# A gated recurrence: transfers of half the image, step by step, and a step's sums in units of 64 columns

## Chip, core and metric

The kernel runs on one core of a Trainium2 chip. The metric is the device time of one execution in microseconds. Five engines run their own instruction streams: TensorE (PE, with its weight loads as PEld), VectorE (DVE), ScalarE (ACT), GpSimd (POOL) and SyncE (SP, which here only issues transfers).

## What is computed

An attention layer and then a GRU, both with a residual, for 4 sequences of 512 positions with 512 features:

```python
x = x + attention_layer(x, cond)         # RMS norm, q, k, v, 16 heads, output projection
# GRU over the 512 positions of x, started from cond:
gi = x @ W_ih + b_ih                     # known for all positions in advance
gh = h @ W_hh + b_hh                     # needs the last state
r = sigmoid(i_r + h_r)
z = sigmoid(i_z + h_z)
n = tanh(i_n + r * h_n)
h = (1.0 - z) * n + z * h                # 512 steps, one after the other
out = x + hs
```

The state of a step is 4 x 512, the weights W_hh are 512 x 1536, all in 32-bit floats.

## The kernel before

The attention stage runs first, then the recurrence: T = 512 steps in N_BLK = 16 blocks of BLK = 32 steps. All engines run the same unrolled loop over the steps and meet through semaphores.

**A step on TensorE** (L490 to L501). The state is the stationary operand (4 columns), the weights stream as the moving one. Four column groups j of 32 columns work on four pieces of the output features side by side. `hidden_side` (L456) makes 8 matmuls for one half of the contraction (2 k by 4 j) over 128 columns; a matmul in 32-bit floats stands in the trace as two loads and two matmuls. The state comes in halves: A (features 0 to 255, semaphore h_a) and B (h_b). After h_a: the first half of the reset sums of all chunks, and of the update and candidate sums (zn) of the A chunks. After h_b: their second halves (r_sum, zna_sum), then both halves of zn for the B chunks (znb_sum). That is 6 calls. Sums are added onto PSUM banks that ScalarE's `seed` (L608) has filled with the input side and the biases, two steps ahead, in alternating triples of banks.

**A step on VectorE and ScalarE.** VectorE transposes the reset sums (L829), ScalarE makes r of them (L625 tanh, L628 affine). VectorE transposes zn of A (L809), adds i_n + r * h_n with a scan (L814), makes z from ScalarE's tanh (L634, L820), ScalarE takes the candidate's tanh (L636), and a scan (L824) writes the new A half. Then the same for B. VectorE's and ScalarE's queues run in this written order.

**The input side.** TensorE computes gi for the next block of 32 steps in pieces (`gi_piece`, L444), one piece after a step's sums, in 24 of 32 steps. VectorE evacuates it with the bias to `gi_image`, three operations of 128 columns for each of 4 sequences (L779, L781). SP writes the image to DRAM (`gi_spill`) and reads it back in another layout into `seeds`, a ring of 44 steps, of which `seed` takes one row set a step. `send_gi` (L202 on) does this once a block: one write of 1536 KB, then for two waves of 16 steps four reads each (8 where the ring wraps), 8 partitions by 16 steps by 1536 bytes. Half of each row set is padding: the candidate's input part stands on other partitions (rows B to 2B) than the rest. Finished blocks go to `out` by `send_rows`; TensorE turns their rows (L485) and ScalarE copies them (L614).

Of the kernel before, what the change touches and what calls it, by code (L numbers as in the profile page):

```python
# [49 lines left out]
RING = 44  # L50
# [4 lines left out]
WAVE = BLK // 2  # L55
# [3 lines left out]
def attention_gru_kernel(nc, x, cond, W_emb, b_emb, g_norm, W_qkv, g_q, g_k, W_out,  # L59
                         W_ih, W_hh, b_ih, b_hh, out):  # L60
    with ExitStack() as ctx:
# [75 lines left out]
        gi_image = sb("gi_image", [P, 2 * B, GCOL])  # L137
        gi_spill = nc.dram_tensor("gi_spill", (P, 2 * B, GCOL), F32, kind="Internal").ap()
# [7 lines left out]

        GI_BANKS, ROW_BANK = (6, 7), 7

        (ld_cond, ld_emb, ld_wqkv, ld_wout, ld_wih, ld_whh, ld_bias, ld_gi_early, ld_gi_late, ld_x, ld_g, st_gi, st_out) = (
            sem(n) for n in ("ld_cond", "ld_emb", "ld_wqkv", "ld_wout", "ld_wih", "ld_whh", "ld_bias", "ld_gi_early", "ld_gi_late",  # L150
# [8 lines left out]
            "bias_ready", "image_clear", "seeds_clear", "hid_n_ready", "pairs_ready", "banks_open", "gi_done", "gi_evac", "seeded", "h_a", "h_b",  # L159
            "r_sum", "zna_sum", "znb_sum", "rT_ready", "znaT_ready", "znbT_ready", "tr_done", "r_ready_gru", "va_done", "vb_done",  # L160
            "tza_done", "tzb_done", "za_done", "zb_done", "na_done", "nb_done", "out_added", "rows_ps", "rows_ready")}

        def step_banks(step):
            first = 3 * (step % 2)
            return first, first + 1, first + 2

        def seed_parts(wave):
            first = wave * WAVE % RING
            count = min(WAVE, RING - first)
            done = wave % 2 * WAVE  # L170
# [18 lines left out]
        def _(sp):  # L189
# [12 lines left out]
            def send_gi(n):  # L202
                sp.wait_ge(s["gi_evac"], 3 * B * (n + 1))
                if n > 0:
                    sp.wait_ge(ld_gi_early, gi_landed(2 * n - 2))
                    sp.wait_ge(ld_gi_late, gi_landed(2 * n - 1))
                sp.dma_start(gi_spill, gi_image[:]).then_inc(st_gi, 16)
                sp.wait_ge(st_gi, 16 * (n + 1))
                for wave in (2 * n, 2 * n + 1):
                    if n > 0:  # L210
                        sp.wait_ge(s["seeded"], (wave + 1) * WAVE - RING)
                    for first, done, count in seed_parts(wave):
                        for j in range(4):
                            sp.dma_start(seeds[QD * j:QD * j + 2 * B, first:first + count, :],
                                         gi_spill[QD * j + done:QD * j + done + count].rearrange("t r n -> r t n")
                                         ).then_inc(ld_gi[wave % 2], 16)

            def send_rows(m):
                sp.wait_ge(s["rows_ready"], KT * (m + 1))
                for b in range(B):  # L220
                    sp.dma_start(out[b, m * BLK:m * BLK + BLK, :], out_rows[BLK * b:BLK * b + BLK, :]).then_inc(st_out, 16)

            sp.wait_ge(s["seeds_clear"], 2)
            send_gi(0)
            for m in range(N_BLK):
                if m + 1 < N_BLK:
                    send_gi(m + 1)
                if m > 0:
                    send_rows(m - 1)
            send_rows(N_BLK - 1)  # L230
# [424 lines left out]
        def _(dve):  # L655
# [141 lines left out]
            for n, b in ((0, 0), (0, 1), (0, 2), (0, 3), (1, 0)):  # L797
                dve.wait_ge(s["gi_done"], B * n + b + 1)
                if n == 1:
                    dve.wait_ge(st_gi, 16)  # L800
# [90 lines left out]
```

## Time and profile before

| | us |
|---|---|
| median of 3 executions | 2526.01 |
| lowest, highest | 2499.19, 2531.39 |
| profiled execution | 2524.64 |
| its span in the trace | 2522.4 |
| TensorE busy | 2255.0 |
| VectorE busy | 1512.3 |
| ScalarE busy | 1245.4 |

The span runs from the first to the last recorded instruction; some 2 us lie outside it. Busy times can overlap, and a busy TensorE is not an array at its peak, since matmuls are pipelined. "Issue" as the reason of a wait means that the engine waited for nothing that the profile shows. DMA queues are numbered; the one called q8 has the kind "instruction".

### The profile page before, as it was taken

The numbers are of one execution on the slowest core, as the hardware profiler recorded it, in microseconds if no ns is written. First come the engines' busy times: TensorE is split into PE (matmuls) and PEld (weight loads), VectorE is DVE, ScalarE is ACT, GpSimd is POOL, SyncE is SP. The second block draws the span as 40 slices with busy tenths as digits, with TensorE's granted clock in tenths as the row PEclk, the third lists the DMA queues.
The fourth block names the chain that finished last, engine by engine and source line by source line (L and its number), as shares of the span: only waits on it lengthen the run. The fifth ranks groups of instructions, "written<-read, shape, count | busy, mean of one in ns | idle before, by whom it ended". The sixth has DMA issues, their size and how long they took to land.

```text
span 2522.4 us, 130844 instructions
## 1 busy us (share of the span) xinstructions
PE 2255.0 (89%) x58512; PEld 1764.2 (70%) x58512; DVE 1512.3 (60%) x5877; ACT 1245.4 (49%) x4666; POOL 199.8 (8%) x223
## 2 busy tenths in 40 slices
PE   5999999998679899989799897979898989979788
PEld 4756666575468687767678685868686778768676
DVE  3867868686256565646466564646565656546565
ACT  3757757574145444444345443545444445445454
POOL 3324232332000000000000000000000000000000
PEclk9999999999799999989899998999999999999999
DMA  5000000001220303021111303030302112030300
GB/s 192 2 18 1 2 17 2 1 2 51 52 53 5 58 5 58 29 33 36 25 41 22 54 9 53 9 57 5 58 32 30 37 25 49 14 55 7 58 4 12
DMA packets 33218, 80.23 MB, mean 32 GB/s; under 512 B 7696, under 2 KB 24080, under 8 KB 30608
## 3 DMA queue, kind: packets, MB, share of 16 engines
q1 hardware_dynamic: 26240, 63.97, 13.0%
q8 instruction: 460, 7.54, 1.3%
q0 software_dynamic: 1584, 7.73, 0.8%
q14 instruction: 102, 0.84, 0.1%
q10 hardware_dynamic: 4832, 0.15, 0.1%
HBM read 42.48 MB, written 29.36 MB: 28 GB/s over the span
## 4 chain that ended last, share of the span: by engine, by line
PE 77%; issue 8%; DVE 7%; ACT 6%; DMA 1%; ACTq 1%; POOL 0%; POOLq 0%; SPq 0%; DVEq 0%
PE ps L461 51%; PE ps L447 6%; PE ps L341 6%; PE ps L292 5%; PE ps L385 2%; PE ps L368 2%; DVE rT L829 2%; PE ps L327 2%; PE ps L434 2%; DVE xb L824 2%; ACT xb L636 1%; ACT r_pair L628 1%; ACT r_pair L625 1%; DVE v_pair L814 1%; ACT probs L595 1%
## 5 line engine op out<-in xcount | busy, mean ns | idle before, releaser
L461 PE MATMUL ps<-wqkv,xb 128*4 128x128 f32 x49152 | 1534.1, 277 | 192.4 <-issue 128.8
L461 PEld LDWEIGHTS ps<-wqkv,xb 128*4 128x4 f32 x49152 | 1240.0, 88 | 493.1 <-DVE xb L824 296.7
L829 DVE STREAM_TRANSPOSE rT<-ps 128x128 f32<-128x128 f32 x512 | 162.2, 317 | 495.5 <-PE ps L461 495.3
L625 ACT ACTIVATE r_pair<-rT 128x16 f32<-128x16 f32 x512 | 112.2, 219 | 653.4 <-DVE rT L829 653.4
L809 DVE STREAM_TRANSPOSE znT<-ps 128x128 f32<-128x128 f32 x1024 | 313.1, 306 | 90.3 <-PE ps L461 30.7
L634 ACT ACTIVATE t_z<-znT 128x8 f32<-128x8 f32 x1024 | 214.5, 209 | 280.1 <-DVE znT L809 279.8
L824 DVE TENSOR_TENSOR_SCAN xb<-z_trip,xb 128x24 f32<-128x24 f32 x1024 | 213.2, 208 | 121.5 <-ACT xb L636 3.6
L609 ACT ACTIVATE ps<-seeds 128x384 f32<-128x384 f32 x512 | 243.9, 476 | 60.3 <-DMA seeds<-gi_spill 60.3
L636 ACT ACTIVATE xb<-v_pair 128x16 f32<-128x16 f32 x1024 | 222.8, 218 | 52.7 <-DVE v_pair L814 0.9
L447 PE MATMUL ps<-wih,x1T 128*32 128x256 f32 (+1 forms) x4096 | 238.1, 328 | 11.3 <-issue 11.3
L814 DVE TENSOR_TENSOR_SCAN v_pair<-r_pair,znT 128x16 f32<-128x16 f32 x1024 | 196.3, 192 | 70.8 <-ACT r_pair L628 0.5
L820 DVE TENSOR_SCALAR z_trip<-t_z 128x8 f32<-128x8 f32 x1024 | 177.8, 174 | 26.5 <-ACT t_z L634 1.0
L341 PE MATMUL ps<-wqkv,xnT 128*128 128x384 f32 x512 | 192.7, 497 | 0.0
L595 ACT ACTIVATE probs<-ps,negmax 128x512 f32<-128x512 f32 x256 | 173.3, 686 | 19.5 <-DVE negmax L725 19.5
L725 DVE TENSOR_REDUCE negmax<-ps 128x1 f32<-128x512 f32 x256 | 158.4, 681 | 8.8 <-PE ps L368 8.8
L292 PEld LDWEIGHTS ps<-ident,probs 128*128 128x128 f32 x1024 | 117.1, 142 | 44.9 <-issue 17.2
L292 PE MATMUL ps<-ident,probs 128*128 128x128 f32 x1024 | 142.3, 279 | 4.0 <-ACT probs L595 3.7
L447 PEld LDWEIGHTS ps<-wih,x1T 128*32 128x32 f32 x4096 | 124.9, 111 | 18.8 <-issue 13.4
L628 ACT ACTIVATE r_pair<-r_pair 128x16 f32<-128x16 f32 x512 | 112.4, 219 | 16.2
L341 PEld LDWEIGHTS ps<-wqkv,xnT 128*128 128x128 f32 x512 | 87.0, 191 | 31.8
L272 POOL TENSOR_TENSOR qk_rs<-qk_ms,half_neg 128x8 f32<-128x8 f32 x64 | 106.7, 1667 | 12.1 <-POOL qk_ms L270 12.1
L729 DVE COPY probsT<-ps 128x512 f32<-128x512 f32 x128 | 82.6, 685 | 36.0 <-PE ps L292 34.3
(83 smaller groups left out, 1266.6 us busy)
## 6 DMA issues: line engine op xcount, KB each, us to landing
gi_spill<-gi_image SPq DMA_DIRECT2D x16, 1536.0 KB, 6.3
seeds<-gi_spill SPq DMA_DIRECT2D x92, 192.0 KB
xb<-in_x SPq DMA_DIRECT2D x4, 1024.0 KB, 5.7
out<-xb SPq DMA_DIRECT2D x64, 64.0 KB, 1.9
seeds<-gi_spill SPq DMA_DIRECT2D x24, 144.0 KB
wqkv<-in_L_cond_W_qkv SPq DMA_DIRECT2D x1, 3072.0 KB, 12.1
wih<-in_L_cond_W_ih POOLq DMA_DIRECT2D x1, 3072.0 KB, 16.4
wqkv<-in_L_cond_W_hh POOLq DMA_DIRECT2D x1, 3072.0 KB, 10.5
```

The source lines that it names most:

```text
L292: return nc.tensor.transpose(dst, src, ident[:])
L341: return nc.tensor.matmul(ps[:, pj(n), 0:3 * P], xnT[:, k, P * t:P * t + P], wqkv[:, k, :].rearrange("p (a g n) -> p a g n", a=3, g=G)[:, ...
L447: last = nc.tensor.matmul(ps[QD * j:QD * j + QD, bank, first:first + width], x1T[:, k, b, BLK * block_no:BLK * block_no + BLK], gate_cols( ...
L461: last = nc.tensor.matmul(ps[QD * j:QD * j + B, bank, 0:P], hist_flat[:, first:first + 3 * B - 2:3], weights, start=False, stop=False, ski ...
L595: nc.scalar.activation(probs[:, hh, :], ps[:, SC[hh], :], ACT.Exp, bias=negmax[:, m % 2, hh:hh + 1], accum_out=sums[:, m % 2, hh:hh + 1]). ...
L609: nc.scalar.activation(ps[:, 3 * (step % 2):3 * (step % 2) + 3, 0:P], seeds[:, step % RING, :].rearrange("p (u n) -> p u n", u=3), ACT.Cop ...
L634: nc.scalar.activation(t_z[:, half, :], znT[:, half, 0:16:2], ACT.Tanh, scale=0.5).then_inc(s[tz_name], 1)
L636: nc.scalar.activation(elements(step, half).rearrange("p (e s) -> p e s", s=3)[:, :, 0:3:2], v_pair[:, 8 * half:8 * half + 8, 1].unsqueeze ...
L809: return nc.vector.transpose(znT[:, half, :].rearrange("p (r k b s) -> p k r s b", r=4, k=4, b=B, s=2), ps[:, bank, 0:P])
L814: return nc.vector.tensor_tensor_scan(v_pair[:].rearrange("p e s -> p (e s)")[:, first:first + 16], r_pair[:].rearrange("p e s -> p (e s)" ...
L824: return nc.vector.tensor_tensor_scan(next_elements(step, half), z_trip[:].rearrange("p e s -> p (e s)")[:, 24 * half:24 * half + 24], ele ...
L829: nc.vector.transpose(rT[:], ps[:, r_bank, 0:P]).then_inc(s["rT_ready"], 1)
```

## The change

*Order of sums.* The step's sums are made in smaller units: reset for the A chunks and for the B chunks are apart (64 columns each), update and candidate of A stay together (128 columns), candidate of B and update of B are apart (64 each). After h_a: r_a, r_b and zn_a, first halves. After h_b: the second halves of r_a, zn_a, r_b, then both halves of n_b (after a wait for raT_ready) and of z_b (after a wait for znaT_ready), since they share a bank with sums that VectorE reads. These are 10 calls of `hidden_side`. VectorE transposes five pieces instead of three, and makes r of the B half itself (affine) from ScalarE's tanh. ScalarE takes the B half's update tanh last. `seed` becomes three copies of 128 elements.

*Image.* `gi_image` holds 4 rows instead of 8, without padding; one evacuation of 384 columns for each sequence. It is written to DRAM sequence by sequence (196 KB each), into one of two buffers. It is read back in four waves of 8 steps, one of the 16 pieces (wave, j) a step, each as two transfers (4 partitions by 8 steps by 1024 bytes, and by 512 bytes). The ring has 36 steps; its candidate part is filled with the hidden bias once. A block's output goes out one sequence a step.

```diff
-RING = 44
+RING = 36
 HIST = 16
 ENTRY = 3 * 17
 GCOL = 3 * P
 LEAD = 12
-WAVE = BLK // 2
+WAVE = 8
+FETCH_LEAD = 17
...
+        gi_spill = nc.dram_tensor("gi_spill", (2, B, P, GCOL), F32, kind="Internal").ap()
...
+        def gate_sums(step):
+            bank = 3 * (step % 2)
+            return {"zn_a": ps[:, bank, 0:2 * HP], "z_b": ps[:, bank, 2 * HP:3 * HP],
+                    "r_a": ps[:, bank + 1, 0:HP], "n_b": ps[:, bank + 1, HP:2 * HP], "r_b": ps[:, bank + 2, 0:HP],
+                    "r_both": ps[:, bank + 1:bank + 3, 0:HP], "n_both": ps[:, bank:bank + 2, HP:2 * HP],
+                    "z_both": ps[:, bank, 0:4 * HP].rearrange("p (h n) -> p h n", h=2)[:, :, 0:HP]}
...
-            def send_gi(n):
-                sp.wait_ge(s["gi_evac"], 3 * B * (n + 1))
-                if n > 0:
-                    sp.wait_ge(ld_gi_early, gi_landed(2 * n - 2))
-                    sp.wait_ge(ld_gi_late, gi_landed(2 * n - 1))
-                sp.dma_start(gi_spill, gi_image[:]).then_inc(st_gi, 16)
-                sp.wait_ge(st_gi, 16 * (n + 1))
-                for wave in (2 * n, 2 * n + 1):
-                    if n > 0:
-                        sp.wait_ge(s["seeded"], (wave + 1) * WAVE - RING)
-                    for first, done, count in seed_parts(wave):
-                        for j in range(4):
-                            sp.dma_start(seeds[QD * j:QD * j + 2 * B, first:first + count, :],
-                                         gi_spill[QD * j + done:QD * j + done + count].rearrange("t r n -> r t n")
-                                         ).then_inc(ld_gi[wave % 2], 16)
-
-            def send_rows(m):
+            def spill(n, b):
+                sp.wait_ge(s["gi_evac"], B * n + b + 1)
+                if n >= 2 and b == 0:
+                    for wave in range(4):
+                        sp.wait_ge(ld_gi[wave], gi_landed(n - 2, wave))
+                sp.dma_start(gi_spill[n % 2, b], gi_image[:, b, :]).then_inc(st_gi, 16)
+
+            def fetch(n, wave, j):
+                for first, done, count in seed_parts(n, wave):
+                    rows = slice(QD * j + done, QD * j + done + count)
+                    sp.dma_start(seeds[QD * j:QD * j + B, first:first + count, 0:2 * P],
+                                 gi_spill[n % 2, :, rows, 0:2 * P]).then_inc(ld_gi[wave], 16)
+                    sp.dma_start(seeds[QD * j + B:QD * j + 2 * B, first:first + count, 2 * P:3 * P],
+                                 gi_spill[n % 2, :, rows, 2 * P:3 * P]).then_inc(ld_gi[wave], 16)
...
+            for step in range(T):
+                m, u = divmod(step, BLK)
+                n, due = divmod(step + FETCH_LEAD, BLK)
+                if 1 <= n < N_BLK and due < 16:
+                    wave, j = divmod(due, 4)
+                    if due == 0:
+                        sp.wait_ge(st_gi, 16 * B * (n + 1))
+                    sp.wait_ge(s["seeded"], step + 2)
+                    fetch(n, wave, j)
+                ahead, due = divmod(step + LEAD - 7, BLK)
+                if ahead + 1 < N_BLK and due % 6 == 0 and due < 6 * B and step + LEAD - 7 >= 6:
+                    spill(ahead + 1, due // 6)
...
-                        last = nc.tensor.matmul(ps[QD * j:QD * j + B, bank, 0:P],
-                                                hist_flat[:, first:first + 3 * B - 2:3], weights,
+                        last = nc.tensor.matmul(into[QD * j:QD * j + B], hist_flat[:, first:first + 3 * B - 2:3], weights,
...
-                hidden_side(r_bank, R_GATE, ALL_CHUNKS, step, 0)
-                hidden_side(zna_bank, ZN_GATES, CHUNKS_A, step, 0)
+                hidden_side(into["r_a"], R_GATE, CHUNKS_A, step, 0)
+                hidden_side(into["r_b"], R_GATE, CHUNKS_B, step, 0)
+                hidden_side(into["zn_a"], ZN_GATES, CHUNKS_A, step, 0)
                 pe.wait_ge(s["h_b"], step + 1)
-                hidden_side(r_bank, R_GATE, ALL_CHUNKS, step, 1).then_inc(s["r_sum"], 1)
-                hidden_side(zna_bank, ZN_GATES, CHUNKS_A, step, 1).then_inc(s["zna_sum"], 1)
-                hidden_side(znb_bank, ZN_GATES, CHUNKS_B, step, 0)
-                hidden_side(znb_bank, ZN_GATES, CHUNKS_B, step, 1).then_inc(s["znb_sum"], 1)
+                hidden_side(into["r_a"], R_GATE, CHUNKS_A, step, 1).then_inc(s["ra_sum"], 1)
+                hidden_side(into["zn_a"], ZN_GATES, CHUNKS_A, step, 1).then_inc(s["zna_sum"], 1)
+                hidden_side(into["r_b"], R_GATE, CHUNKS_B, step, 1).then_inc(s["rb_sum"], 1)
+                pe.wait_ge(s["raT_ready"], step + 1)
+                hidden_side(into["n_b"], N_GATE, CHUNKS_B, step, 0)
+                hidden_side(into["n_b"], N_GATE, CHUNKS_B, step, 1).then_inc(s["nb_sum"], 1)
+                pe.wait_ge(s["znaT_ready"], step + 1)
+                hidden_side(into["z_b"], Z_GATE, CHUNKS_B, step, 0)
+                hidden_side(into["z_b"], Z_GATE, CHUNKS_B, step, 1).then_inc(s["zb_sum"], 1)
...
-                nc.scalar.activation(ps[:, 3 * (step % 2):3 * (step % 2) + 3, 0:P],
-                                     seeds[:, step % RING, :].rearrange("p (u n) -> p u n", u=3),
-                                     ACT.Copy).then_inc(s["seeded"], 1)
+                into, image = gate_sums(step), seeds[:, step % RING, :]
+                halves = lambda ap: ap.rearrange("p (h n) -> p h n", h=2)
+                nc.scalar.activation(into["r_both"], halves(image[:, 0:P]), ACT.Copy)
+                nc.scalar.activation(into["z_both"], halves(image[:, P:2 * P]), ACT.Copy)
+                nc.scalar.activation(into["n_both"], halves(image[:, 2 * P:3 * P]), ACT.Copy).then_inc(s["seeded"], 1)
...
+                act.wait_ge(s["raT_ready"], step + 1)
+                nc.scalar.activation(by_chunk(t_r[:, 0, :]), of_rows(rT[:, 0:HP]), ACT.Tanh, scale=0.5).then_inc(s["tra_done"], 1)
+                act.wait_ge(s["tra_done"], step + 1)
+                nc.scalar.activation(r_pair[:, 0:8, 1], t_r[:, 0, :], ACT.Copy, bias=0.5, scale=0.5).then_inc(s["ra_ready"], 1)
+                act.wait_ge(s["znaT_ready"], step + 1)
+                nc.scalar.activation(t_z[:, 0, :], znT[:, 0, 0:16:2], ACT.Tanh, scale=0.5).then_inc(s["tza_done"], 1)
+                act.wait_ge(s["rbT_ready"], step + 1)
+                nc.scalar.activation(by_chunk(t_r[:, 1, :]), of_rows(rT[:, HP:P]), ACT.Tanh, scale=0.5).then_inc(s["trb_done"], 1)
+                act.wait_ge(s["va_done"], step + 1)
+                candidate_tanh(0).then_inc(s["na_done"], 1)
+                act.wait_ge(s["vb_done"], step + 1)
+                candidate_tanh(1).then_inc(s["nb_done"], 1)
+                act.wait_ge(s["zbT_ready"], step + 1)
+                nc.scalar.activation(by_chunk(t_z[:, 1, :]), of_rows(znT[:, 1, HP:P]), ACT.Tanh, scale=0.5).then_inc(s["tzb_done"], 1)
...
+                nc.vector.tensor_tensor(gi_image[:, b, :], ps[:, GI_BANKS[b % 2], 0:GCOL], b_in[:],
+                                        ALU.add).then_inc(s["gi_evac"], 1)
...
+                dve.wait_ge(s["ra_sum"], step + 1)
+                nc.vector.transpose(rT[:, 0:HP], into["r_a"]).then_inc(s["raT_ready"], 1)
                 dve.wait_ge(s["zna_sum"], step + 1)
-                transpose_zn(0, zna_bank).then_inc(s["znaT_ready"], 1)
-                dve.wait_ge(s["r_ready_gru"], step + 1)
+                nc.vector.transpose(znT[:, 0, :].rearrange("p (r k b s) -> p k r s b", r=4, k=4, b=B, s=2),
+                                    into["zn_a"]).then_inc(s["znaT_ready"], 1)
+                dve.wait_ge(s["rb_sum"], step + 1)
+                nc.vector.transpose(rT[:, HP:P], into["r_b"]).then_inc(s["rbT_ready"], 1)
                 dve.wait_ge(s["znaT_ready"], step + 1)
-                candidate(0).then_inc(s["va_done"], 1)
+                dve.wait_ge(s["ra_ready"], step + 1)
+                candidate(0, znT[:, 0, 16:32]).then_inc(s["va_done"], 1)
                 dve.wait_ge(s["tza_done"], step + 1)
-                z_gate(0).then_inc(s["za_done"], 1)
+                affine(z_trip[:, 0:8, 2], t_z[:, 0, :]).then_inc(s["za_done"], 1)
+                dve.wait_ge(s["nb_sum"], step + 1)
+                nc.vector.transpose(znT[:, 1, 0:HP].rearrange("p (r k b s) -> p k r s b", r=4, k=2, b=B, s=2),
+                                    into["n_b"]).then_inc(s["nbT_ready"], 1)
+                dve.wait_ge(s["trb_done"], step + 1)
+                affine(r_pair[:, 8:16, 1], t_r[:, 1, :]).then_inc(s["rb_ready"], 1)
                 dve.wait_ge(s["na_done"], step + 1)
                 dve.wait_ge(s["za_done"], step + 1)
                 new_state(0).then_inc(s["h_a"], 1)
 
-                dve.wait_ge(s["znb_sum"], step + 1)
-                transpose_zn(1, znb_bank).then_inc(s["znbT_ready"], 1)
-                dve.wait_ge(s["znbT_ready"], step + 1)
-                candidate(1).then_inc(s["vb_done"], 1)
+                dve.wait_ge(s["rb_ready"], step + 1)
+                dve.wait_ge(s["nbT_ready"], step + 1)
+                candidate(1, znT[:, 1, 0:16]).then_inc(s["vb_done"], 1)
+                dve.wait_ge(s["zb_sum"], step + 1)
+                nc.vector.transpose(znT[:, 1, HP:P], into["z_b"]).then_inc(s["zbT_ready"], 1)
                 dve.wait_ge(s["tzb_done"], step + 1)
-                z_gate(1).then_inc(s["zb_done"], 1)
+                affine(z_trip[:, 8:16, 2], t_z[:, 1, :]).then_inc(s["zb_done"], 1)
+                dve.wait_ge(s["zb_done"], step + 1)
                 dve.wait_ge(s["nb_done"], step + 1)
-                dve.wait_ge(s["zb_done"], step + 1)
                 new_state(1).then_inc(s["h_b"], 1)
```

## Rows read from the trace of the kernel before

**Rows 1.** The page: busy time, and shares of the chain that ended last
```profile
PE 2255.0 (89%) x58512; PEld 1764.2 (70%) x58512; DVE 1512.3 (60%) x5877; ACT 1245.4 (49%) x4666; POOL 199.8 (8%) x223
...
PE ps L461 51%; PE ps L447 6%; PE ps L341 6%; PE ps L292 5%; PE ps L385 2%; PE ps L368 2%; DVE rT L829 2%; PE ps L327 2%; PE ps L434 2%; DVE xb L824 2%; ACT xb L636 1%; ACT r_pair L628 1%; ACT r_pair L625 1%; DVE v_pair L814 1%; ACT probs L
```

**Rows 2.** Window of the recurrence: us, PE, PEld, DVE, ACT, POOL busy, PEclk, DMA
```profile
664.00:2514.00 1850.00, 1663.67 (x53276) 1360.79 (x53268) 1063.52 (x4871) 850.46 (x3636) 0.00 (x0) 0.96 0.17 32
```

**Rows 3.** Timeline, 1500 to 1516 us: start, us, engine, line, op, [idle before <-releaser]
```profile
1502.43 1.64 PEld L461 LDWEIGHTS ps<-wqkv,xb 128*4 128x4 f32 x64 [0.20 <-DVE xb L824]
1503.12 0.32 DVE L829 STREAM_TRANSPOSE rT<-ps 128x128 f32<-128x128 f32 x1 [0.56 <-PE ps L461]
1503.47 0.22 ACT L625 ACTIVATE r_pair<-rT 128x16 f32<-128x16 f32 x1 [0.99 <-DVE rT L829]
...
1504.18 0.62 PE L447 MATMUL ps<-wih,x1T 128*32 128x256 f32 x8
...
1505.42 0.21 DVE L824 TENSOR_TENSOR_SCAN xb<-z_trip,xb 128x24 f32<-128x24 f32 x1
...
1505.68 1.64 PEld L461 LDWEIGHTS ps<-wqkv,xb 128*4 128x4 f32 x64 [0.20 <-DVE xb L824]
...
1513.94 0.62 PE L447 MATMUL ps<-wih,x1T 128*32 128x128 f32 x16
```

**Rows 4.** Waits, weight loads, 664 to 2514 us: total us, times, longest
```profile
PEld ps L461 <- issue: 138.5, 34, 10.6
PEld ps L447 <- issue: 12.5, 4, 8.3
```

**Rows 5.** DMA queues, 664 to 2514 us: packets, MB, share of 16 engines
```profile
q8 instruction: 418, 6.85, 1.6%
```

**Rows 6.** DMA queues, 1534.9 to 1562.5 us, the image on its way
```profile
q1 hardware_dynamic: 1116, 1.57, 51.5%
q8 instruction: 3, 0.05, 1.1%
```

**Rows 7.** Timeline, 1543.5 to 1566.5 us, weight loads at two long waits
```profile
1553.98 3.90 PEld L461 LDWEIGHTS ps<-wqkv,xb 128*4 128x4 f32 x81 [9.90 <-issue]
...
1564.78 1.82 PEld L461 LDWEIGHTS ps<-wqkv,xb 128*4 128x4 f32 x39 [5.32 <-issue]
```

**Rows 8.** Windows, between these two waits
```profile
1553.90:1559.60 5.70, 5.61 (x127) 4.06 (x128) 2.08 (x9) 1.87 (x8) 0.00 (x0) 0.68 0.56 60
```

**Rows 9.** DMA rate, 1564.7 to 1572.7 us, in 40 slices of 0.2 us
```profile
GB/s 0 0 0 0 0 0 82 0 0 0 0 0 0 0 0 0 0 0 0 0 0 0 0 0 0 0 0 0 82 0 0 0 0 0 0 0 0 0 0 0
```

**Rows 10.** DMA rate in slices of 0.15 us, and queues, 2333 to 2339 us
```profile
GB/s 0 0 0 0 109 0 0 0 0 0 0 0 0 0 0 0 0 0 0 0 0 0 0 0 0 0 0 0 0 0 0 0 109 0 0 0 0 0 0 0
...
q8 instruction: 2, 0.03, 2.9%
```

**Rows 11.** Timeline, weight loads, 2331 to 2339.5 us
```profile
2336.59 0.97 PEld L461 LDWEIGHTS ps<-wqkv,xb 128*4 128x4 f32 x35 [0.65 <-issue]
```

**Rows 12.** Groups by line and shape: busy us, mean ns | idle before
```profile
L461 PE MATMUL ps<-wqkv,xb 128*4 128x128 f32 x49152 | 1534.1, 277 | 192.4 <-issue 128.8 <-DVE xb L824 38.3 <-ACT ps L609 17.6
...
L609 ACT ACTIVATE ps<-seeds 128x384 f32<-128x384 f32 x512 | 243.9, 476 | 60.3 <-DMA seeds<-gi_spill 60.3
...
L829 DVE STREAM_TRANSPOSE rT<-ps 128x128 f32<-128x128 f32 x512 | 162.2, 317 | 495.5 <-PE ps L461 495.3
L447 PE MATMUL ps<-wih,x1T 128*32 128x256 f32 x2048 | 160.5, 383 | 7.8 <-issue 7.8
...
L614 ACT ACTIVATE xb<-ps 128x128 f32<-128x128 f32 x64 | 16.2, 259 | 2.1 <-PE ps L485 2.1
...
L674 DVE STREAM_TRANSPOSE sq<-ps 128x256 f32<-128x256 f32 x1 | 0.4, 429 | 0.0
```

**Rows 13.** Timeline, 625 to 672 us: first image and first seeds
```profile
645.15 3.18 SPq L214 DMA_DIRECT2D seeds<-gi_spill  x8
...
661.10 0.91 ACT L609 ACTIVATE ps<-seeds 128x384 f32<-128x384 f32 x2 [60.27 <-DMA seeds<-gi_spill]
```

More of the change, by code:

```diff
@@ L230, in _ @@
-            send_rows(N_BLK - 1)
+            for b in range(B):
+                spill(0, b)
+            sp.wait_ge(st_gi, 16 * B)
+            for wave in range(4):
+                for j in range(4):
+                    fetch(0, wave, j)
+            spill(1, 0)
+            for step in range(T):
[10 more added lines that the diff above has]
+                    spill(ahead + 1, due // 6)
+                if m > 0 and 24 <= u < 24 + B:
+                    send_rows(m - 1, u - 24)
@@ L231, in _ @@
+            for b in range(B):
+                send_rows(N_BLK - 1, b)
             sp.wait_ge(st_out, 16 * B * N_BLK)
@@ L454, in _, with hidden_side @@
             PIECES = [[(k, GATES_RZ)] for k in range(KT)] + [[(0, GATE_N), (1, GATE_N)], [(2, GATE_N), (3, GATE_N)]]
-            def hidden_side(bank, gates, chunks, step, half):
+            def hidden_side(into, gates, chunks, step, half):
                 for k in (2 * half, 2 * half + 1):
@@ L630, in _ @@
-                for half, names in ((0, ("znaT_ready", "tza_done", "va_done", "na_done")),
-                                    (1, ("znbT_ready", "tzb_done", "vb_done", "nb_done"))):
-                    transposed, tz_name, v_name, n_name = names
-                    act.wait_ge(s[transposed], step + 1)
-                    nc.scalar.activation(t_z[:, half, :], znT[:, half, 0:16:2], ACT.Tanh, scale=0.5).then_inc(s[tz_name], 1)
-                    act.wait_ge(s[v_name], step + 1)
-                    nc.scalar.activation(elements(step, half).rearrange("p (e s) -> p e s", s=3)[:, :, 0:3:2],
-                                         v_pair[:, 8 * half:8 * half + 8, 1].unsqueeze(2).broadcast_to([P, 8, 2]),
-                                         ACT.Tanh).then_inc(s[n_name], 1)
+                of_rows = lambda ap: ap.rearrange("p (c r) -> p c r", r=QD)[:, :, 0:B]
@@ L795, in add_out, with candidate @@
                 last.then_inc(s["out_added"], 1)
+            dve.wait_ge(s["bias_ready"], 1)
             for n, b in ((0, 0), (0, 1), (0, 2), (0, 3), (1, 0)):
-                dve.wait_ge(s["gi_done"], B * n + b + 1)
-                if n == 1:
-                    dve.wait_ge(st_gi, 16)
-                for part in range(3):
-                    evacuate_gi(b, part, GI_BANKS[b % 2])
+                evacuate_gi(n, b)
             for step in range(T):
                 m, u = divmod(step, BLK)
-                r_bank, zna_bank, znb_bank = step_banks(step)
-                def transpose_zn(half, bank):
-                    return nc.vector.transpose(
-                        znT[:, half, :].rearrange("p (r k b s) -> p k r s b", r=4, k=4, b=B, s=2), ps[:, bank, 0:P])
-                def candidate(half):
+                into = gate_sums(step)
+                def candidate(half, gates):
                     first = 16 * half
```

120 lines of the change are left out of this document (50 added, 70 removed).

## The prediction

> **What bounds the kernel now.** I read the page first: TensorE is busy for 89% of the span, and the chain that ended last runs through L461 for half of it [rows 1]. That is no proof that the array is the limit, so the stages come next. The attention stage, before 664 us, is left alone by the change; 664 to 2514 us is the recurrence, 512 steps in 1850 us, or 3.61 us a step [rows 2]. A step in a quiet stretch takes 3.25 us (the weight loads for the B half start at 1502.43 and again at 1505.68) [rows 3]. 512 x 3.25 is 1664 us, so some 186 us of the stage are something else: the waits put down to "issue" on the loads of L461 and L447, 138.5 and 12.5 us [rows 4], and steps slowed after them.
>
> The quiet step is a ring: 0.69 us from the first B load to the reset transpose, then transpose, tanh, affine, scan, tanh, scan for the A half and transpose, scan, tanh, scan for the B half, which ends at 1505.63, 0.05 us before the next load [rows 3]. TensorE's work fits beside it, just: 64 loads take 1.64 us, so a record takes 25.6 ns, and they come in four column groups side by side, a set of four each 0.10 to 0.11 us.
>
> The "issue" waits say what the second limit is. Queue q8 moved 418 packets of 16 KB in the recurrence [rows 5], and TensorE ran 53,276 matmuls and 53,268 loads in it [rows 2]: 106,544 / 418 = 255 records a packet, with the wait instructions 256. So q8 brings TensorE's program in blocks of 256 instructions. Between the two long waits at 1553.98 and 1564.78 the engine ran 127 matmuls and 128 loads [rows 7, 8]: one block, then nothing. It had at most the next block in hand. While the image moved (1.57 MB, 27.6 us) only 3 blocks came [rows 6], where quiet steps of 418 x 256 / 512 = 209 instructions ask for one per 4.0 us.
>
> How fast can blocks come when nothing is in the way? After the engine entered a block at 1564.78 the next packet began in the seventh 0.2 us slice, so 1.1 to 1.3 us later [rows 9]. A packet occupies its queue 1.6% x 16 x 1850 / 418 = 1.13 us in the mean [rows 5]. From the end of a packet to the first instruction out of it: in a window with no other traffic one began at 2333.6 to 2333.75, the two there took 2.9% x 16 x 6 / 2 = 1.4 us each, and TensorE, idle for 0.65 us on "issue", resumed at 2336.59 [rows 10, 11]. That leaves 1.44 us at least, 1.6 at most. The next packet began at 2337.80 to 2337.95, so here, with slow packets, blocks were 4.2 us apart. With the mean packet, and the near edge of each slice: 1.1 + 1.13 + 1.4 = 3.63 us. Bounds: 3.2 us (1.1, 0.9 and 1.2, each piece taken somewhat short of these rows, an estimate) and 4.2 us.
>
> **The change, part by part.** *Matmuls.* L461 has 49,152 matmuls [rows 12], 96 a step: six calls of 8 matmuls in the code, two records each. The new order makes r_a, r_b, n_b and z_b two calls each at 64 columns and zn_a two at 128: ten calls, 160 records. Array time hardly moves if a set scales with its columns, and it does here: 8 matmuls of 256 columns and 16 of 128 both take 0.62 us [rows 3]. Eight sets at 0.109 and thirty-two at 0.055 are 2.63 us, against 24 x 0.109 = 2.62. But the instructions grow by 64 matmuls and 64 loads a step, 65,536 in all, and these are 256 more blocks: 418 + 256 = 674. A step becomes 674 x 256 / 512 = 337 instructions. At 3.63 us a block it can't be shorter than 4.78 us.
>
> *The ring.* I walked it with the rows' durations. A 64-column sum closes 0.2 us earlier: three short sets for three long ones save 0.16 us, and its own stream is shorter by half of the 106 ns that separates the 383 ns (256 columns) and 277 ns (128) forms [rows 12]. A 64-column transpose is 0.26 us by the line through 317 ns (128) and 429 ns (256) [rows 12]. From the first B load: ra transposed at 0.73, zn_a at 1.23, rb at 1.37, candidate scan A at 1.53, tanh A at 1.78, n_b transposed at 1.88, state A at 2.14 (before: 2.23), scan B at 2.31, z_b transposed at 2.50, tanh z at 2.74 behind tanh B on ScalarE, affine at 2.95, state B at 3.26, next load 3.31. VectorE has three transposes of 0.26 and one of 0.32 in place of three of about 0.3, and one more affine: what the shorter reset wins, its queue gives back. So the ring stays 3.3 us, bounds 3.25 and 3.37 (transposes of 0.20 and 0.317). The ring alone would be +0.03 x 512 = 25 us.
>
> *Waits on PE.* n_b waits for raT_ready, z_b for znaT_ready; behind them queue all later matmuls. By the walk raT is there at 0.73 and the array reaches n_b at 0.89; znaT at 1.23 and z_b at 1.33. Price nothing while the sums keep this order; if that cover is gone, 0.1 us a step, 51 us.
>
> *Seeds and evacuations.* One ScalarE copy of 384 elements (476 ns) becomes three of 128 (259 ns for such a copy from PSUM) [rows 12], +0.3 us, in the time in which ScalarE waits for the next reset transpose (1.0 us) [rows 3]. Three evacuations of 0.27 us become one of some 0.5 in every sixth step, in VectorE's idle time before the reset transpose. Nothing on the path.
>
> *Image.* Per 32 steps 1.57 MB in bulk become 0.79 MB, 48 KB a step over 16 steps. SP issues two to four transfers a step; eight took 3.18 us [rows 13], so 0.8 to 1.6 us of a step. The start gains: the first copy waited for a wave of 786 KB, issued from 645.15 and landed by 661.10 [rows 13]; the new first wave is 197 KB, 4 us at that rate, 8 at half of it. Minus 9 us. The long waits go. What stays is a block that finds a transfer ahead of it: 48 KB at 1.57 MB / 27.1 us is 0.85 us, 1.7 if four partitions a transfer halve the rate. 16 steps of 4.8 us hold 21 blocks; at 0.3 us each, that is 6.4 us, times 15 images, 96 us. Nearest bounds: 0 (packets elsewhere than the blocks) and 21 x 1.7 x 15 = 535 us. I take 100, since the transfer stands in the way less than half of the time.
>
> **Sum**, against the profiled execution (2524.64 us, within 0.1% of the median): start 664 - 9 = 655; 674 x 3.63 = 2447; contention 100; tail 2522.4 - 2514 = 8.4; outside the span 2.2. Together 3213 us, which I round to 3210.
>
> **A rule that speaks against it.** The trace shows a block in hand and one on its way, and waits as soon as a block is late [rows 7, 11]. The Trainium skill, "Runtime: NRT & Kernel Launch", section Instruction fetch mechanics, agrees on blocks of 256 instructions but says that fetching is hidden because instructions issue slower than blocks arrive, and gives TensorE a store of 2048 instructions. By that the step would be the ring's and the total rival A's; a store of eight blocks would have outlasted the 10 us wait in [rows 7], so the trace disagrees.
>
> **Rivals.** *A, blocks do not bind (the other side).* If blocks came faster than my pieces say (below 256 / 337 x 3.31 = 2.5 us), the ring would set the step: 655 + 512 x 3.31 + 10.6 = 2360 us, up to 2450 with leftover waits. For it: nothing in the trace ever asked for more than one block in about 3.6 us. Against: in [rows 10, 11] blocks 4.2 us apart already stopped TensorE with no other traffic. 9%.
> *B, the array has a floor per matmul.* If a set of 64 columns took the 0.109 us of one of 128, the array would need 40 x 0.109 = 4.36, plus 8 to 16 records for the input side, 0.3 us in the mean: 4.7 us a step, 655 + 2406 + 11 = 3072 us, under the block limit, so it changes the total only if A's condition holds too. For it: no row has 64-column sets. 6% as the binding limit. The Trainium skill, "TensorE: Matmul & The Clock Gate" (the section on 56 against 53.3 ns), has matmuls never start closer than about 25 ns; 160 of them are 4.0 us, with the input side 4.3, total about 2870 by that rule. No row here decides it: the present spacing is 25.6 ns.
> *C, contention is as bad as the bound.* 535 instead of 100 us: 3650 us. Against: a block can now only stand behind one step's transfers. 6% beyond 3500.
> *D, the waits on PE turn serial or blocks come at 3.2 us.* 674 x 0.43 less is 2923 us; this is the main case's low end.
>
> **Numbers.** The main case (blocks set the step) has 76% and runs from 2890 to 3500; B adds 6% and C 6% on the slower side. No change would need gains and losses to cancel: 3%. Range 2890 to 3500: it leaves out A, C's far end and the no-change case. 2% is about what a measurement of this kernel can tell from no change. Slower 0.88, same 0.03, faster 0.09.
>
> **What would show it.** Right: about 716 q8 packets in all, in the recurrence one about every 3.6 us in quiet steps; L461 with 81,920 matmuls; "issue" waits of 1 us or so on TensorE more than once a step, of the order of 500 to 700 us in total, instead of few long ones; a recurrence of about 4.8 us a step in the stretches without image traffic too; ScalarE's and VectorE's waits for TensorE grown. Wrong: steps of 3.3 us with few such waits (A), or TensorE's sets of 64 columns 0.1 us apart with no waits on issue (B).

## The result, and the profile after

| | before | after |
|---|---|---|
| median, us | 2524.89 | 3197.95 |
| lowest, highest | 2499.19, 2531.39 | 3188.01, 3201.08 |
| span of the profiled execution | 2522.4 | 3196.7 |

Each median is that of four executions. The ratio is 1.268, interval 1.259 to 1.278. The forecast was 3210, range 2890 to 3500. The page of the changed kernel has the span and instructions, the busy times, the instruction queue, the chain, and the two groups of the hidden side:

```profile
span 3196.7 us, 200394 instructions
...
PE 2295.9 (72%) x91328; PEld 1892.6 (59%) x91328; DVE 1537.5 (48%) x7281; ACT 1354.4 (42%) x6202; POOL 203.4 (6%) x223
...
q8 instruction: 716, 11.73, 1.6%
...
PE 66%; issue 27%; DVE 3%; ACT 2%; DMA 1%; ACTq 0%; POOLq 0%; POOL 0%; SPq 0%; DVEq 0%
...
L482 PE MATMUL ps<-wqkv,xb 128*4 128x64 f32 (+1 forms) x81920 | 1631.2, 230 | 794.7 <-issue 777.1
L482 PEld LDWEIGHTS ps<-wqkv,xb 128*4 128x4 f32 x81920 | 1421.1, 87 | 1000.8 <-issue 911.2
```

TensorE is busy for about as long as before, 2296 against 2255 us, in a span 674 us longer. "Issue" has grown from 8 to 27% of the chain; before, the same line read:

```profile
PE 77%; issue 8%; DVE 7%; ACT 6%; DMA 1%; ACTq 1%; POOL 0%; POOLq 0%; SPq 0%; DVEq 0%
```

The window of the recurrence (columns as in [rows 2]), its waits of the weight loads, and its queues:

```profile
653.00:3187.00 2534.00, 1705.72 (x86002) 1489.11 (x85994) 1093.59 (x6288) 958.81 (x5169) 0.00 (x0) 1.00 0.06 16
```
```profile
PEld ps L482 <- issue: 905.4, 639, 2.1
```
```profile
q1 hardware_dynamic: 29481, 27.85, 3.6%
q8 instruction: 673, 11.03, 1.9%
```

The recurrence takes 2534 us, 4.95 a step, for 1850 and 3.61 before [rows 2]. Where 34 waits of up to 10.6 us stood in [rows 4], there are 639, none above 2.1 us: the image's long waits are gone, and short ones in every step are there. (2534.00 / 673 is one block in 3.77 us.) The timeline of the weight loads, for three blocks of 256 instructions (of the first, its opening line):

```profile
1659.81 0.82 PEld L482 LDWEIGHTS ps<-wqkv,xb 128*4 128x4 f32 x58 [1.42 <-issue]
...
1663.70 1.76 PEld L482 LDWEIGHTS ps<-wqkv,xb 128*4 128x4 f32 x107 [1.68 <-issue]
1665.71 0.32 PEld L482 LDWEIGHTS ps<-wqkv,xb 128*4 128x4 f32 x20 [0.25 <-DVE xb L850]
1667.61 2.24 PEld L482 LDWEIGHTS ps<-wqkv,xb 128*4 128x4 f32 x128 [1.58 <-issue]
```

From 1663.70 the engine runs 107 + 20 loads, one block with their matmuls, and stops; at 1667.61, 3.91 us later, it runs 128 and stops again. It executes a block in 2.2 to 2.4 us and stands for 1.4 to 1.7. What a late block makes wait next is seen in the timeline at 1702 us:

```profile
1702.26 2.21 PEld L482 LDWEIGHTS ps<-wqkv,xb 128*4 128x4 f32 x128 [1.62 <-issue]
...
1703.40 0.25 DVE L855 STREAM_TRANSPOSE rT<-ps 128x64 f32<-128x64 f32 x1 [2.06 <-PE ps L482]
1703.68 0.21 ACT L663 ACTIVATE t_r<-rT 128x8 f32<-128x8 f32 x1 [2.23 <-DVE rT L855]
```

### The profile page after: what moved, and what is told of

Read it like the earlier page. It is cut to its first block, busy times and chain, and to the rows that moved or that the text cites. A ratio compares the mean times of both kernels' runs of the same rounds, so it can differ in the third digit from the quotient of the medians.

```text
span 3196.7 us, 200394 instructions
## 1 busy us (share of the span) xinstructions
PE 2295.9 (72%) x91328; PEld 1892.6 (59%) x91328; DVE 1537.5 (48%) x7281; ACT 1354.4 (42%) x6202; POOL 203.4 (6%) x223
## 4 chain that ended last, share of the span: by engine, by line
PE 66%; issue 27%; DVE 3%; ACT 2%; DMA 1%; ACTq 0%; POOLq 0%; POOL 0%; SPq 0%; DVEq 0%
PE ps L482 45%; PE ps L468 5%; PE ps L362 5%; PE ps L313 4%; PE ps L406 2%; PE ps L389 2%; PE ps L348 2%; PE ps L455 1%; ACT probs L623 1%; PE ps L507 1%; DVE xb L850 1%; POOLq L62 0%; DVE znT L857 0%; DVE z_trip L847 0%; DVE r_pair L847 0%
## 5 line engine op out<-in xcount | busy, mean ns | idle before, releaser
L482 PE MATMUL ps<-wqkv,xb 128*4 128x64 f32 (+1 forms) x81920 | 1631.2, 230 | 794.7 <-issue 777.1
L482 PEld LDWEIGHTS ps<-wqkv,xb 128*4 128x4 f32 x81920 | 1421.1, 87 | 1000.8 <-issue 911.2
L855 DVE STREAM_TRANSPOSE rT<-ps 128x64 f32<-128x64 f32 x512 | 128.0, 250 | 677.2 <-PE ps L482 674.3
L663 ACT ACTIVATE t_r<-rT 128x8 f32<-128x8 f32 x512 | 106.9, 209 | 793.2 <-DVE rT L855 793.2
L468 PE MATMUL ps<-wih,x1T 128*32 128x256 f32 (+1 forms) x4096 | 261.3, 326 | 35.2 <-issue 33.7
L857 DVE STREAM_TRANSPOSE znT<-ps 128x128 f32<-128x128 f32 x512 | 162.7, 318 | 174.3 <-PE ps L482 174.3
L879 DVE STREAM_TRANSPOSE znT<-ps 128x64 f32<-128x64 f32 x512 | 121.8, 238 | 186.3 <-PE ps L482 185.8
L867 DVE STREAM_TRANSPOSE znT<-ps 128x64 f32<-128x64 f32 x512 | 127.4, 249 | 158.9 <-PE ps L482 155.0
L860 DVE STREAM_TRANSPOSE rT<-ps 128x64 f32<-128x64 f32 x512 | 120.3, 235 | 85.9 <-PE ps L482 85.9
L639 ACT ACTIVATE ps<-seeds 128x128 f32<-128x128 f32 x512 | 134.6, 263 | 51.0 <-DMA seeds<-gi_spill 51.0
L669 ACT ACTIVATE t_r<-rT 128x8 f32<-128x8 f32 x512 | 106.8, 209 | 88.7 <-DVE rT L860 88.7
## 6 DMA issues: line engine op xcount, KB each, us to landing
wqkv<-in_L_cond_W_hh POOLq DMA_DIRECT2D x1, 3072.0 KB, 10.6
```

What stands on the lines that cost most here:

```text
L468: last = nc.tensor.matmul(ps[QD * j:QD * j + QD, bank, first:first + width], x1T[:, k, b, BLK * block_no:BLK * block_no + BLK], gate_cols( ...
L482: last = nc.tensor.matmul(into[QD * j:QD * j + B], hist_flat[:, first:first + 3 * B - 2:3], weights, start=False, stop=False, skip_group_c ...
L639: nc.scalar.activation(into["r_both"], halves(image[:, 0:P]), ACT.Copy)
L857: nc.vector.transpose(znT[:, 0, :].rearrange("p (r k b s) -> p k r s b", r=4, k=4, b=B, s=2), into["zn_a"]).then_inc(s["znaT_ready"], 1)
```

## The experiments

Every ratio is to the kernel before, in runs beside it on the same chip. In these runs the kernel before had medians of 2509 to 2513 us, somewhat less than the 2524.89 us above, and the ratios go by those.

### The two halves of the change, each alone

`image_only`: the new image, its transfers and evacuation, with before's six calls and before's queues of VectorE and ScalarE; its `seed` is three copies, as in the changed kernel. `order_only` is the reverse.

```diff
# image_only, against the changed kernel: a step's sums as before
+                hidden_side(r_bank, R_GATE, ALL_CHUNKS, step, 0)
+                hidden_side(zna_bank, ZN_GATES, CHUNKS_A, step, 0)
                 pe.wait_ge(s["h_b"], step + 1)
+                hidden_side(r_bank, R_GATE, ALL_CHUNKS, step, 1).then_inc(s["r_sum"], 1)
...
# order_only, against the changed kernel: ring, waves and transfers as before
+RING = 44
+WAVE = BLK // 2
...
+                sp.dma_start(gi_spill, gi_image[:]).then_inc(st_gi, 16)
```

> The image part alone: half-size, paced transfers with the order of sums as before. Theory P (blocks of 256 instructions, one per 3.77 us as in the profile after): 209 instructions a step ask for 418 blocks, 1576 us, less than the ring's 512 x 3.25 = 1664 us, so the ring sets the step and the long waits are gone: 653 + 1664 + 11 = 2330 us, up to 2380 with short waits in steps of 226 to 242 instructions. Rival R (the new order's own chain or array work is slow, blocks are a symptom): the same 2330 to 2380. Rival I (the paced transfers slow everything): over 3000 us.

> The new order of sums with the image in bulk as before. Theory P: 674 blocks at 3.77 us are 2541 us, plus the long waits of the bulk image, 10 to 13 us for each of 15 images, 150 to 200 us: 664 + 2541 + 175 + 11 = 3390 us, more than the kernel with both parts. If pacing is worth nothing in this regime: 3216 us. Rival I (the loss comes from the paced transfers): about 2550 us.

`image_only` took 2335.35 us (2332.81 to 2335.78), ratio 0.930, interval 0.924 to 0.935. `order_only` took 3345.78 us (3330.38 to 3362.9), ratio 1.332, interval 1.323 to 1.342. The window of `image_only`'s recurrence, then a step's B loads and reset transpose in its timeline, then the waits of `order_only`'s loads:

```profile
653.00:2325.00 1672.00, 1624.33 (x53326) 1338.07 (x53320) 1056.42 (x4754) 943.65 (x4659) 0.00 (x0) 1.00 0.07 21
```
```profile
1702.91 1.64 PEld L477 LDWEIGHTS ps<-wqkv,xb 128*4 128x4 f32 x64 [0.21 <-DVE xb L838]
1703.34 0.34 SPq L209 DMA_DIRECT2D gi_spill<-gi_image  x1
1703.61 0.32 DVE L843 STREAM_TRANSPOSE rT<-ps 128x128 f32<-128x128 f32 x1 [0.30 <-PE ps L477]
```
```profile
PEld ps L467 <- issue: 1006.5, 623, 19.5
```

The new image is worth 174 us by itself against the 2509.32 us beside it (190 against 2524.89), by the traces 1850 - 1672 = 178 us of recurrence and 11 us of an earlier start: 1672 / 512 is 3.27 us a step, the quiet step of [rows 3], nearly everywhere, and the reset transpose starts 0.70 us after the first B load, as there. The new order costs 3197.95 - 2335.35 = 863 us on top of the new image. With the old image it costs more: `order_only` is 148 us above the changed kernel. Of the distances from one of its instruction packets to the next, 541 had at most 16 KB of other traffic in them and a mean of 3.72 us, 132 had more and a mean of 4.95 us; 132 x 1.23 is 162 us, of the size of that difference.

### The instructions alone

`pad32` is `image_only` with 32 extra matmuls a step, each over four columns of a constant, added into a part of a bank that is filled anew before it is used. They add 65,536 instructions, 256 blocks, as many as the new order does. The pads also wait for `seeded`, but no wait of theirs is put down to it. `pad16` and `pad8` have 16 and 8 of them, 128 and 64 blocks more.

```diff
+                pe.wait_ge(s["seeded"], min(step + 2, T))
+                for i in range(32):
+                    j = i % 4
+                    nc.tensor.matmul(ps[QD * j:QD * j + B, 3 * ((step + 1) % 2), P:P + 4], ident[:, 0:B], ident[:, 0:4],
+                                     start=False, stop=False, skip_group_check=True, tile_position=(0, QD * j))
```

> The image part with the old order, and 32 matmuls of 4 columns a step behind the sums, on constants, whose results nobody reads: 64 loads and 64 matmuls more a step, the same number of instructions as in the changed kernel, with hardly any array time and nothing of the new order. Theory P: 674 blocks, 653 + 2541 + 11 = 3205 us, as the changed kernel. Rival R (order, ring or the array's 64-column sets are what is slow): the pads cost at most some 0.5 us of array time a step, so 2600 us at most. Rival F (a floor of 25 ns per matmul): 64 x 0.025 = 1.6 us a step less the idle time of 0.1 to 0.3, about 3030 us.

> As pad8 with 16 matmuls: 64 instructions more a step. Theory P: 546 blocks at 3.74 us, 2042 us, 653 + 2042 + 11 = 2706 us. Array time shared evenly over the pads: 2335 + 423 = 2758 us. Between pad8 and pad16 theory P wants 239 us, between pad16 and pad32 478 us.

> As pad32 with 8 matmuls of 4 columns a step: 32 instructions more a step. Theory P (a straight line in the number of instructions once blocks bind; 3.74 us a block as in pad32): 418 + 64 = 482 blocks, 1803 us, 653 + 1803 + 11 = 2467 us, up to 2490. A theory in which pads cost array time (the 846 us of pad32 over the image part alone, shared evenly over 32 pads): 2335 + 212 = 2547 us. If neither: 2335 us.

| kernel | blocks | us | ratio, interval |
|---|---|---|---|
| image_only | 418 | 2335.35 | 0.930, 0.924 to 0.935 |
| pad8 | 482 | 2469.60 | 0.985, 0.979 to 0.991 |
| pad16 | 546 | 2702.88 | 1.079, 1.072 to 1.085 |
| pad32 | 674 | 3176.24 | 1.263, 1.254 to 1.273 |
| changed kernel | 674 | 3197.95 | 1.268, 1.259 to 1.278 |

The window of `pad32`'s recurrence, and its waits:

```profile
656.00:3175.00 2519.00, 1959.91 (x86030) 1767.18 (x86018) 1069.73 (x4758) 944.79 (x4660) 0.00 (x0) 1.00 0.06 16
```
```profile
PEld ps L477 <- issue: 445.6, 383, 1.9
...
PEld ps L524 <- issue: 214.5, 256, 1.6
```

`pad32` has the old order, the old shapes of the sums and four-column additions, and comes within 22 us of the changed kernel. The number of TensorE instructions is enough to make the time; 64-column sets, the waits on raT_ready and znaT_ready, and VectorE's five transposes are not needed for it. Theory P's figures for the pads (3205, 2706 and 2467 us) came out within 1%. From `pad16` on a block costs (3176.24 - 2702.88) / 128 = 3.70 us, from `pad8` to `pad16` 3.65. From none to `pad8` it costs 2.10: the first blocks go into what room there was. That is the knee of a second limit that rises past the ring. The knee alone doesn't say which limit: array time, or a floor of 25 ns for each matmul (rival F of the expectation), could have one too. The pads' own time rules these out:

```profile
1700.66 0.59 PEld L524 LDWEIGHTS ps<-ident 128*4 128x4 f32 x48
...
1702.05 0.16 PEld L524 LDWEIGHTS ps<-ident 128*4 128x4 f32 x16 [0.81 <-issue]
```

48 pad loads with their matmuls take 0.59 us, 12 ns each, then TensorE stands for 0.81 us in the middle of the pads. All pad loads together are busy for 412 us, 0.80 us a step, where a step has grown by (3176.24 - 2335.35) / 512 = 1.64 us.

### The new order with fewer instructions

`after_short` is the changed kernel without the first halves of r_a, r_b, zn_a and z_b. Four of ten calls are gone, and with them 65,536 instructions, so that it has the 418 blocks of before; those sums lack half of their terms.

```diff
-                hidden_side(into["r_a"], R_GATE, CHUNKS_A, step, 0)
-                hidden_side(into["r_b"], R_GATE, CHUNKS_B, step, 0)
-                hidden_side(into["zn_a"], ZN_GATES, CHUNKS_A, step, 0)
...
-                hidden_side(into["z_b"], Z_GATE, CHUNKS_B, step, 0)
```

> The changed kernel with four of the ten calls left out: the first halves (contraction over the A features) of r_a, r_b, zn_a and z_b, so the sums lack these terms. The waits, VectorE's and ScalarE's work and the path from h_b to the state stay; three of the four calls lay in the wait for h_b. 128 instructions less a step leave 209. Theory P: 418 blocks, 1576 us, no longer the limit; the new ring shows itself: by my walk 3.31 us a step, 653 + 1695 + 11 = 2360 us. Rival R (the new ring or VectorE's queue is slow by itself): near 3198 us, at least over 2700.

It took 2403.98 us (2396.41 to 2414.42), ratio 0.958, interval 0.951 to 0.964: 44 us more than expected, with the ring shorter than expected. One step in its timeline:

```profile
1701.68 1.58 PEld L482 LDWEIGHTS ps<-wqkv,xb 128*4 128x4 f32 x96 [1.36 <-issue]
...
1702.18 0.25 DVE L851 STREAM_TRANSPOSE rT<-ps 128x64 f32<-128x64 f32 x1 [0.62 <-PE ps L482]
...
1703.51 0.20 DVE L846 TENSOR_TENSOR_SCAN xb<-z_trip,xb 128x24 f32<-128x24 f32 x1
1703.64 0.19 DVE L837 TENSOR_TENSOR_SCAN v_pair<-r_pair,znT 128x16 f32<-128x16 f32 x1
1703.75 0.23 DVE L875 STREAM_TRANSPOSE znT<-ps 128x64 f32<-128x64 f32 x1
...
1704.46 0.21 DVE L846 TENSOR_TENSOR_SCAN xb<-z_trip,xb 128x24 f32<-128x24 f32 x1
...
1704.78 1.23 PEld L482 LDWEIGHTS ps<-wqkv,xb 128*4 128x4 f32 x68 [1.38 <-issue]
```

The ring closes in 3.10 us (1701.68 to 1704.78), 0.15 less than in the kernel before. The wait called "issue" here is the ordinary one for the B state: the load starts 0.11 us after the scan's end at 1704.67, so the sum of this row's kind is no measure of late blocks. But only two steps in five take 3.10 us; the median is 3.2 and the mean 3.39. A step of 3.10 us has room for 3.10 / 3.70 x 256 = 214 instructions, where most steps have some 209 and those with 16 input-side matmuls some 225, so the block limit is close. The packets bear it out: for 170 of the 418, TensorE resumes 1.25 to 1.5 us after the packet's end, for 56 in `image_only`, which waits for no block and meets that stretch by chance, and for 526 of 673 in the changed kernel. A smaller part is the clock, which was 0.98 in the mean:

```profile
653.00:2386.00 1733.00, 1133.70 (x53283) 929.00 (x53275) 1074.55 (x6286) 947.86 (x5169) 0.00 (x0) 0.98 0.07 21
```

27 steps that lie in part in stretches at half clock took 4.19 us in the mean, the others 3.34, some 23 us in all. No run takes the two apart.

### What in the image made the long waits

Four kernels with before's order: half the bytes in two bursts of eight pieces (`half_two`, 393 KB a burst); the full 1.57 MB one piece a step (`paced_full`); the full 1.57 MB as the same small pieces in two bursts of 786 KB (`full_two`); and, with the half image, the reset affine on VectorE (`image_dve_r`), a part of the new order that adds no TensorE instruction.

```diff
# half_two, against image_only
-                if 1 <= n < N_BLK and due < 16:
-                    wave, j = divmod(due, 4)
+                if 1 <= n < N_BLK and due in (0, 12):
...
+                    for wave in ((0, 1), (2, 3))[due // 12]:
+                        for j in range(4):
+                            fetch(n, wave, j)
...
# paced_full, against the kernel before: pieces of 8 steps, one a step
+            for step in range(T):
...
+                n, due = divmod(step + 15, BLK)
+                if 1 <= n < N_BLK and due < 16:
...
+                    fetch(n, due // 4, due % 4)
...
# full_two, against paced_full
-                if 1 <= n < N_BLK and due < 16:
+                if 1 <= n < N_BLK and due in (0, 8):
...
# image_dve_r, against image_only
-                nc.scalar.activation(r_pair[:, :, 1], r_pair[:, :, 1], ACT.Copy, bias=0.5,
-                                     scale=0.5).then_inc(s["r_ready_gru"], 1)
...
+                dve.wait_ge(s["tr_done"], step + 1)
+                nc.vector.tensor_scalar(r_pair[:, :, 1], t_r[:], 0.5, 0.5, ALU.mult, ALU.add).then_inc(s["r_ready_gru"], 1)
```

> The image part alone, but unpaced: the half-size image is fetched in two bursts a block of steps, 8 of the 16 pieces each (393 KB), at the steps at which the first and the thirteenth piece were due. If pacing made the gain (a block behind a burst waits for most of it, 7 to 13 us, less what is in hand): two long waits per image, 31 x 3 to 6 us, 2430 to 2520 us. If halving made it: within 1% of the 2335 us of the paced form.

> The kernel before with its full image (1.57 MB, with padding, one write), but fetched in 16 pieces of 8 steps (98 KB), one a step. If pacing alone removes the long waits: start as before at 664 us, 664 + 1664 + 11 = 2339 us, up to 2360. If the amount counts (a piece of 98 KB drains at 57 GB/s in 1.7 us and the image's write stays): some short waits, 2360 to 2420. If neither: 2513 us.

> As paced_full, but in two bursts of 8 pieces (786 KB each), 8 steps apart: the same small pieces as the paced form, unpaced, with the full amount. If the size of one transfer was what counts: as paced_full, about 2340 us. If the backlog counts (a burst is issued in 3 us and drains in 14): long waits as before, 2430 to 2520 us.

> The image part alone, with the affine of the reset gate on VectorE behind the zn transpose instead of on ScalarE: no instruction more on TensorE. Theory P says that this kernel is bound by the ring, so a shorter ring shows in full: affine 0.13 us instead of 0.22 (the r_pair affine of the short kernel against ScalarE's), 0.05 to 0.09 us a step, 26 to 46 us: 2290 to 2310 us. If TensorE's blocks were already the limit (418 x 3.74 = 1563 us, a step of 3.05 us), the floor is 2227 us, not reached here.

| with before's order | us | ratio, interval |
|---|---|---|
| full image in bulk (the kernel before) | 2524.89, beside these 2509 to 2513 | 1 |
| full image, small pieces, two bursts | 2447.27 | 0.975, 0.970 to 0.981 |
| full image, a piece a step | 2358.89 | 0.940, 0.934 to 0.946 |
| half image, two bursts | 2334.06 | 0.930, 0.927 to 0.933 |
| half image, a piece a step | 2335.35 | 0.930, 0.924 to 0.935 |
| the same, reset affine on VectorE | 2332.84 | 0.930, 0.927 to 0.933 |

Waits of TensorE's matmuls in the recurrence, first of `paced_full`, then of `full_two`, and the queues of `half_two` in the 14 us around one burst:

```profile
PE ps L469 <- issue: 10.3, 12, 2.5
```
```profile
PE ps L471 <- issue: 68.0, 22, 8.2
```
```profile
q1 hardware_dynamic: 768, 0.66, 18.7%
q8 instruction: 3, 0.05, 1.5%
```

With the full image the pacing counts: 88 us between `full_two` and `paced_full`, and the waits for blocks are 68 us against 10. With the half image it counts for nothing, and the expectation for `half_two` missed by some 100 us. In its burst SP issues a transfer every 0.35 us and the queue drains about as they come; three blocks arrive in those 14 us, and the longest distance of two blocks in its recurrence is 5.55 us, as in `image_only` (5.61). For the full image it is shown that the backlog makes blocks late, since `full_two` and `paced_full` differ only in when the same transfers are issued. That the half image has no such backlog is measured, but not why: against `full_two`, `half_two` changes the bytes, the transfers' shape and their packets, and it also writes the image in four parts. Nor is the step from the kernel before to `full_two` (63.5 us against the 2510.77 beside it) taken apart: its transfers are smaller, and its write and its two bursts stand apart in time.

`image_dve_r` missed its expectation too: a shorter ring was expected, and it takes 2.5 us less than `image_only`, within the spread of either. Its timeline:

```profile
1701.54 0.32 DVE L841 STREAM_TRANSPOSE rT<-ps 128x128 f32<-128x128 f32 x1 [0.30 <-PE ps L478]
...
1701.98 0.32 DVE L821 STREAM_TRANSPOSE znT<-ps 128x128 f32<-128x128 f32 x1
1702.22 0.13 DVE L846 TENSOR_SCALAR r_pair<-t_r 128x16 f32<-128x16 f32 x1
1702.33 0.21 ACT L652 ACTIVATE t_z<-znT 128x8 f32<-128x8 f32 x1 [0.22 <-DVE znT L821]
1702.40 0.19 DVE L826 TENSOR_TENSOR_SCAN v_pair<-r_pair,znT 128x16 f32<-128x16 f32 x1
```

The affine stands behind the transpose of zn in VectorE's queue; the scan begins 0.86 us after the reset transpose, as in the kernel before.

## Why the prediction was right, and where its terms were off

**The limit.** Right. It was read from one row of 0.65 us of "issue" in quiet traffic [rows 11], from one block between two long waits [rows 8] and from the packet count [rows 5]. `pad32` shows it as a cause: it has the new image, which alone made the kernel faster, and nothing of the new order but the number of instructions. The step that no block is in hand beyond the next holds too: after each wait in the timelines above the engine gets 127 or 128 loads and is dry. So the Trainium skill's sentence ("Runtime: NRT & Kernel Launch", Instruction fetch mechanics) that fetching is hidden does not describe this kernel. What the same section says elsewhere, that the next block of 256 is fetched while the present one runs, the trace agrees with: the next packet begins 1.24 us after TensorE resumes, while it still runs its block. But from one block to the next it takes 3.77 us, and TensorE runs a block in 2.2 us.

**The count of blocks.** 716 in all and 673 in the recurrence, as forecast (716, 674); L482 has the 81,920 matmuls.

**The time of a block, undersized.** 3.63 was forecast, 3.77 measured. The trace after, over 650 blocks: 1.24 us from resuming to the next packet (forecast 1.1), 1.14 us for the packet (1.13), 1.38 us from its end to the next instruction (1.4). I took the near edge of a slice for the first; its far edge was 1.3. 674 x 0.14 is 94 us too little.

**Contention, oversized.** 100 was forecast; it is nothing that can be seen. Blocks with other traffic beside them came every 3.76 us, those without every 3.77. The step that failed is that a block would find a transfer of 48 KB ahead of it and stand behind it for 0.3 us in the mean: these distances show no such delay. `half_two` agrees, where even eight pieces at a time pass without a long wait, though there the ring left the blocks some 0.3 us of room each. The two errors, -94 and +100, cancelled. The sum came out within 12 us, but its terms are only good to 100.

**The ring, oversized.** 3.31 was walked, `after_short` measures 3.10 where nothing is late. The prediction's price for it, +0.03 x 512 = 25 us, was also a slip: 3.31 against 3.25 is 0.06 x 512 = 31 us. The walk let VectorE's operations follow one another at their full durations. They overlap: the candidate scan starts 0.13 us after the state scan of 0.20, and the transpose of z_b 0.11 after that scan of 0.19. `after_short` has z_b's first half missing, 4 sets or 0.22 us; its loads end at 1703.26, 0.49 us before that transpose, so the missing half would still fit in. The term did not bind in the sum. It does in rival A: without the block limit the new order would take about 653 + 512 x 3.10 + 11 = 2251 us, less than the kernel before and `image_only`. That is an estimate from a kernel with fewer sums, and not a run.

**The array and the waits on PE.** Sets scale with their columns, which rules out rival B. Groups by line and shape:

```profile
L482 PE MATMUL ps<-wqkv,xb 128*4 128x64 f32 x65536 | 1394.1, 219 | 652.0 <-issue 634.3 <-ACT ps L641 7.1 <-DVE xb L850 4.6
L482 PE MATMUL ps<-wqkv,xb 128*4 128x128 f32 x16384 | 713.8, 273 | 142.7 <-issue 142.7
```

The 64-column form is 54 ns shorter (forecast 53), and 128 loads, four in five of them for such sets, took 2.21 us, 17 ns a record where 25.6 was the spacing before; rival B would have kept the old spacing. The Trainium skill ("TensorE: Matmul & The Clock Gate", the section on 56 against 53.3 ns) has matmuls start no closer than some 25 ns; this trace disagrees, where neighbouring matmuls go to different column groups, and so do the pads at 12 ns. No wait for raT_ready or znaT_ready stands among those of TensorE; price nothing was right, though with blocks late it was hardly tested.

**The size of the issue waits.** 500 to 700 us was forecast, 905 measured. By the forecast's own terms (4.78 - 3.31) x 512 + 100 is 853; that sentence did not follow from them.

**Start and long waits.** The first reset transpose came at 653.0 us instead of 664.5, 11.5 earlier (forecast 9). The long waits went.

## What to carry to other kernels

Count TensorE's instructions in a step: here a step cannot be shorter than its instructions / 256 x 3.7 us, so splitting a sum to start its reader earlier can cost more than all it gains, even though the array's time stays the same. Look for short "issue" waits in stretches without traffic; one of 0.65 us was the sign that the supply was nearly used up. And where blocks are late because of a transfer, the image of half the size was worth at least as much as pacing the full one: the new image with the old order takes 2335 us, 7% less than the kernel before, and is the one to keep.

## What the runs showed of the hardware

A wait of some us costs more than itself, through the clock. Windows of the kernel before around its wait of 5.32 us (PEclk is the third number from the end):

```profile
1564.70:1568.00 3.30, 3.22 (x64) 2.50 (x67) 1.19 (x5) 0.86 (x4) 0.00 (x0) 0.53 0.02 5
1568.00:1572.00 4.00, 4.00 (x130) 3.23 (x125) 2.48 (x11) 2.04 (x9) 0.00 (x0) 1.00 0.02 4
```

After the wait TensorE ran at 0.53 of full speed, near its level of 1.2 GHz, for some 3 us, and then at 2.4 GHz again. That is part of why 151 us of issue waits in [rows 4] stood for some 180 us of the recurrence, which `image_only` gained beside its earlier start. In the changed kernel the granted clock is 1.00 over the whole recurrence, with 639 waits of up to 2.1 us: there they cost no clock. `after_short` has waits of up to 2.4 us and a mean of 0.98, so short waits are not free of it in every kernel.
